# A graph-layer kernel with its ranks moved behind the second filter layer on TensorE, and its places behind the product on VectorE

## What is computed

```
h   = relu(layernorm(x)) @ W_in2f.T
Wij = (smu(edge_attr_20 @ W_f1.T + b_f1) @ W_f2.T + b_f2) * edge_weight[:, None]
agg = segment_sum(h[dst] * Wij, src, num_segments=12500)
out = x + smu(agg @ W_o1.T + b_o1) @ W_o2.T + b_o2
smu(v) = (1.01 v + 0.99 v erf(2.475 v)) / 2
```

## Time and profile before

| | |
|---|---|
| median of 3 runs | 4146.94 us (4142.5 to 4153.49) |
| span of the profiled execution | 5246.4 us |
| TensorE (PE) busy in it | 4105.5 us, 78% |
| VectorE (DVE) busy | 3459.8 us, 66% |
| GpSimd (POOL) busy | 3044.9 us, 58% |
| ScalarE (ACT) busy | 2190.0 us, 42% |
| mean granted TensorE clock | 0.902 of full |

### The profile page before, as it was taken

One profiled execution on the slowest core, in us unless ns is written; L12 is line 12 of the kernel. 1 busy time (PEld: TensorE's weight loads), 2 busy tenths in 40 slices (PEclk: granted clock), 3 DMA queues, 4 the chain that ended last, 5 costly groups with the idle time before them and its releaser, 6 DMA issues.

```text
span 5246.4 us, 97364 instructions
## 1 busy us (share of the span) xinstructions
PE 4105.5 (78%) x23774; PEld 2777.5 (53%) x23774; DVE 3459.8 (66%) x11848; ACT 2190.0 (42%) x7302; POOL 3044.9 (58%) x3173
## 2 busy tenths in 40 slices
PE   6677667777777777777777778788888888887888
PEld 3344335555555555555555555555555666655557
DVE  6666556666666666666666666666666777766677
ACT  4566444444443344444443434434443443334333
POOL 4666655555555555555555555655555555555553
PEclk8888889988988989989889899998888999998999
DMA  6455445554444444444444445554444555554446
GB/s 181 122 147 147 126 118 144 147 144 146 146 133 125 125 124 125 131 127 125 127 126 121 134 145 148 148 153 132 132 133 136 158 157 152 159 160 136 139 137 206
DMA packets 459545, 737.14 MB, mean 141 GB/s; under 512 B 87168, under 2 KB 255466, under 8 KB 459104
## 3 DMA queue, kind: packets, MB, share of 16 engines
q1 hardware_dynamic: 291606, 461.44, 33.5%
q0 software_dynamic: 100000, 206.60, 11.7%
q10 hardware_dynamic: 67626, 65.48, 3.8%
HBM read 465.36 MB, written 267.82 MB: 140 GB/s over the span
## 4 chain that ended last, share of the span: by engine, by line
PE 36%; another core or an unknown queue 25%; DVE 16%; issue 14%; ACT 7%; ACTq 1%; DMA 1%; DVEq 1%; SPq 0%; POOL 0%
PE p_w L1207 7%; PE p_h L1222 7%; PE p_seg L1256 6%; PE p_m L1213 6%; PE p_z L1202 5%; DVE product L1003 4%; DVE hg L995 4%; ACT msg L723 3%; PE p_pos L1244 2%; DVE onehot L988 2%; PE p_pos L1228 2%; DVE act L979 2%; ACT hg L717 2%; DVE pick L983 1%
## 5 line engine op out<-in xcount | busy, mean ns | idle before, releaser
L588 POOL DMA_INDIRECT sorted_rows<-msg,row_idx x3125 | 3004.5, 961 | 2122.6 <-issue 904.5
L1003 DVE CUSTOM_DVE_ANT_0 product<-onehot,p_pos,start_at 128x112 bf16<-128x112 bf16 x3136 | 849.2, 326 | 1096.3 <-remote 1012.3
L723 ACT ACTIVATE msg<-p_m,weight 128x128 f32<-128x128 f32 x3136 | 893.5, 369 | 1439.1 <-remote 786.2
L1256 PEld LDWEIGHTS p_seg<-seg_hot,seg 128*128 128x128 f32 x8288 | 1066.4, 196 | 464.5 <-issue 461.8
L1213 PE MATMUL p_m<-ident,hg 128*128 128x128 f32 x3136 | 561.2, 307 | 905.9 <-DVE hg L995 649.7
L1256 PE MATMUL p_seg<-seg_hot,seg 128*128 128x112 f32 x8288 | 1085.6, 279 | 117.3 <-issue 107.8
L1213 PEld LDWEIGHTS p_m<-ident,hg 128*128 128x128 f32 x3136 | 384.5, 155 | 1102.0 <-DVE hg L995 675.3
L1207 PE MATMUL p_w<-act,w_f 128*128 128x512 f32 x1568 | 932.0, 679 | 10.4 <-issue 5.7
L1202 PE MATMUL p_z<-attr,w_f 128*128 128x512 f32 x1568 | 853.8, 626 | 56.3 <-issue 24.3
L995 DVE SCALAR_TENSOR_TENSOR hg<-p_w,bias_w,hg 128x512 f32<-128x512 f32 x784 | 588.0, 750 | 464.9 <-remote 155.4
L717 ACT COPY hg<-p_h 128x512 f32<-128x512 f32 x784 | 461.9, 589 | 878.4 <-remote 592.3
(11 more groups left out here) (114 smaller groups left out, 2157.8 us busy)
## 6 DMA issues: line engine op xcount, KB each, us to landing
seg<-sorted_rows SPq DMA_DIRECT2D x448, 322.5 KB
seg<-sorted_rows SPq DMA_DIRECT2D x196, 516.0 KB
ends<-ends SPq DMA_DIRECT2D x392, 256.0 KB
sorted_rows<-msg,row_idx POOLq DMA_INDIRECT x3125
sorted_rows<-zero_rows ACTq DMA_DIRECT2D x336, 129.0 KB
win<-h SPq DMA_DIRECT2D x392, 96.0 KB
attr<-in_attrT SPq DMA_DIRECT2D x392, 80.0 KB
seg<-sorted_rows SPq DMA_DIRECT2D x56, 387.0 KB
```

The costliest lines, as they stand in the source:

```text
L588: pool.indirect_dma_start(out=sorted_rows[:, :], out_offset=bass.IndirectOffsetOnAxis(ap=row_idx[:, slot, k:k + 1], axis=0), in_=msg[:, sl ...
L723: last = act.activation(msg[:, slot, k, 0:F], p_m[:, k, :], ACT.Copy, scale=weight[:, bass.ds(n.value(TILES_U, k), 1)])
L1003: last = dve.tensor_tensor_reduce(out=product[:, k, :], in0=onehot[:, slot, k, :], in1=p_pos[:, 0:BUCKETS], scale=1.0, scalar=start_at[:, ...
L1256: last = pe.matmul(out, seg[:, it.slot, l * it.tiles + k, 0:F], seg_hot[:, it.slot, l * it.tiles + k, :], start=(k == 0), stop=(k == it.ti ...
```

## The change

On TensorE `rank(c-1)` goes from ahead of `targets(c-1)` and `filter2(c-1)` to behind them, and a wait for s_w of unit c-1 stands ahead of it: TensorE waits there until the second layer that it has just issued is complete. On VectorE `gather_sum` and `product_of(c-1)` go ahead of `places(c-1)` and `row_numbers(c-1)`. No instruction with work in it is added or removed; 783 beats have the new order (the very first ones are written out apart and stay).

```diff
@@ VectorE, step @@
-                if st.has(1):
-                    places(st.at(1), st.v(1), st.ring(1), st.i is None and st.rnd == 0 and st.c == mid_step + 1)
                 for it in st.items(1):
                     if it.closes:
                         gather_sum(it)
                 if st.has(1):
+                    product_of(st.at(1), st.v(1))
+                    places(st.at(1), st.v(1), st.ring(1), st.i is None and st.rnd == 0 and st.c == mid_step + 1)
                     row_numbers(st.at(1), st.v(1), st.ring(1))
-                    product_of(st.at(1), st.v(1))
@@ TensorE, step @@
                 if st.has(1):
-                    rank(st.at(1), st.ring(1), st.rnd_of(1), st.opens(1))
                     targets(st.at(1), st.pair(1), st.q(1), st.v(1))
                     filter2(st.at(1), st.v(1))
+                    wait_for(pe, s_w, st.at(1), 1, 1)
+                    rank(st.at(1), st.ring(1), st.rnd_of(1), st.opens(1))
```

## The result

The kernel after takes **4156.01 us** (median of 14 runs, 4152.37 to 4161.26) against 4149.12 us for the kernel before in 14 runs: a ratio of **1.0018, 95% interval 1.0011 to 1.0026**. The direction is right, the size is a third of what was forecast.

What follows compares the result with a forecast made beforehand. POOL was taken as the bound, at 5.05 us a unit. To 4147 us came 32 us where PE's beats pass that, less 9 us of lead and 2 us already paid: 4168 us, range 4122 to 4212.

Steps and rivals of the forecast that it cites:

- the floor of 4099 us: Whole run if POOL never waits: 39 us before the first scatter, 3947 of scatters, 113 behind the last.
- The wait's cost: PE's wait between second layer and ranks, in 783 beats: 0.32 us a beat, from 0.20 to 0.45.
- the 0.10 us for the weight load: Part of PE's wait: the ranks' first weight load, 0.10 us ahead of its matmul, is laid bare behind the wait.
- Part 2: New order on PE, ranks behind picked rows and second layer: same matmuls, zero, up to 9 x 0.5 us at round openings.
- The heavy rounds: Seventh and eighth rounds, where PE's beat passes POOL's 5.05 us: 17 us and 15 us.
- The lead that I subtracted: PE's lead over POOL on entering the heavy rounds: covers 9 us of the 32 us excess.
- The gain from the order: Reordering on PE and DVE: both put at zero in the sum.
- faster: Rival: longer lead covers short interruptions, saving half of POOL's 48 us of waits; 4125 us, chance 0.16.
- the 48 us that POOL waits: All waits of POOL before the change: median of 4147 us against 4099 us without waits.
- The gain in lead: Product ahead of row numbers on DVE: PE can run about 3 us further ahead of POOL.
- No change that can be measured: Rival: heavy rounds' 32 us shrink to under 12, within about 0.3%; 4147 us, chance 0.31.
- PE as the bound in most rounds: Rival: a mean clock under about 0.95 lengthens PE's beats; 79 us less 9, 4217 us, chance 0.16.

Runs made afterwards that it cites:

- the slowed GpSimd: Kernel after, with and without TensorE's wait, plus a memset and a wait on GpSimd in each unit: 4748.25 and 4750.6 us, ratios 1.1414 and 1.1421.
- no_wait: Kernel after without TensorE's wait for the second layer, both moves kept: 4138.38 us, ratio 0.9983 to the kernel before.
- wait_heavy: Kernel after with TensorE's wait kept only in the seventh and eighth rounds: 4159.05 us, ratio 1.0006 to the kernel before.
- before_again: Kernel before, unchanged, run again for a second profile: ratio 1.0002, profiled span 4135.8 us.
- dve_only: Kernel before with only the move on VectorE, TensorE's order unchanged and no added wait: 4145.7 us, ratio 0.9998.

## Why the prediction was right or wrong

**The bound was right.** POOL's pitch of 1.263 us, 5.05 us a unit, and the floor of 4099 us came out of a profile that was 26% too long; the clean profiles show the same pitch, and the slowed GpSimd shows the time following it. Taking the durations and not the waits of the first profile was the step that held.

**The wait's cost was too high, and the order's on TensorE was put at zero.** I summed 0.16 + 0.10 + 0.06 = 0.32 us for the wait; measured are 0.22 to 0.23. The term that failed is the 0.10 us for the weight load. The load does start only when the wait is met (3434.05), but the matmul is recorded as starting with it, and the ranks take 0.40 us as before. The Trainium skill, in "TensorE: Matmul & The Clock Gate", section "Step-by-step: what each phase is for", says that TensorE pulls a weight load ahead of matmuls in flight when it goes to the background buffer. By that rule and my other two terms the wait would cost 0.22 us. The number agrees with the trace, but the trace has the load behind the wait and not ahead of it, so it does not show that mechanism. Part 2 gave the new order nothing on TensorE; no_wait shows 0.06 us a beat. The two errors nearly cancel: the eight-tile beat grew by 0.30 us where the sum had 0.32, and that this is close is luck.

**The heavy rounds were mis-sized.** This is the first step that made the forecast too large: TensorE's beat in these rounds was put 0.09 us too long. I had 17 us for the seventh round and 15 for the eighth. The eight-tile beat before is 4.96 us and not 5.03: the transposes of the earlier trace rows, with a wait of TensorE just ahead of them, took 0.49 us, and back to back they take 0.43 or 0.44 (in after from 3437.15 to 3437.58). So the excess over 5.05 us after is 0.21 and not 0.30 us, 12 us in the seventh round; in the eighth, by the medians of its beats (8 of 5.26, 13 of 6.15 and 19 of 4.81 us), the mean is 5.34 us and not 5.43, 11 us. That is 23 us where I had 32. The lead that I subtracted was 9 us; early in the seventh round it is 5.3 us in the trace of after, and the round used it up. With my other terms the sum would have been some 12 us instead of 21. The price of the wait measured by itself is 14.6 us.

By the units' mean lengths in the two profiles (seventh 5.206 before and 5.233 us after, eighth 5.186 and 5.428) the seventh costs 2 us and the eighth 10 us more than before. The split between them is not firm: wait_heavy, with the same order in these rounds, has 5.329 and 5.423. The stop at a late landing just before the eighth round falls into the seventh, with a wait of POOL of 6.5 us in before_again, 3.0 and 2.2 in after, 5.1 in no_wait and 7.3 in wait_heavy. Since after and wait_heavy have the same order and the same wait there, one trace of each can't show that the longer lead shortens it.

**The gain from the order had no term.** This is the second step, a term put at nothing. I put the reordering at zero in the sum and held it for the rival "faster" (4125 us). no_wait shows 7 us of gain, about a seventh of the 48 us that POOL waits, although TensorE's beat is 0.06 us longer in it. 14.6 - 7 = 7.6 us is the measured difference. Where the 7 us arise stays open: POOL's waits over the 0.30 us between scatters add up to 31 us in before_again and 29 in no_wait, and one profile of each, the former of the shortest of its 11 executions, can't tell 5 us. The granted clock is not the reason: its median over the runs is 0.979 before, 0.982 for no_wait and 0.989 for dve_only, which gains nothing.

**The gain in lead was right.** I forecast about 3 us more of it; in the second to fourth rounds p_w is complete a median of 6.1 to 6.3 us before the end of POOL's previous unit, against 3.5 to 3.7 us in before_again. The gain in lead, 2.6 us, is as forecast; the lead with which TensorE enters the heavy stretch of the seventh round was not (5.3 us where I subtracted 9).

**The rivals.** "No change that can be measured" had the right range (within 12 us), by a mixture I had not named: a wait of 0.22 us paid in two rounds, and a gain from the order. PE as the bound in most rounds is refuted: the granted clock is 0.98 to 0.99 of full in the clean profiles, not the 0.87 to 0.90 of the earlier trace rows, which went with the stops of that one execution. The agreement of that rival with the 48 us left over was a coincidence. In before_again 31 us of them are waits of POOL (12 in the first round, 14 in the two heavy rounds, 5 elsewhere) and some 11 us are scatters that follow each other a little later than 1.263 us; the rest lies between this execution and the median. What I had not thought of is that the two moves depend on each other: either side's effect alone is no guide to both (1.0174 and 0.9998 make 1.0018).

## What to carry to other kernels

Find the engine whose instructions stand back to back, and price every change by what it does to that engine's waits: a wait of 0.22 us in 783 beats costs nothing that can be measured in 687 of them and 14 us in the 96 where the beat is as long as the bound. Work out beat lengths round by round, since the length of most beats (4.6 against 5.05 us here) hides the rounds that pay, and take them from beats that follow each other without idle time: the 0.06 us by which one beat was read too long was a fifth of the excess. When work is moved later on one engine, look for what stands ahead of the critical instruction on the engine that consumes it: the ranks behind the second layer cost 1.7% until the product had been moved ahead of the places.

## What the runs showed of the hardware

One profiled execution was 26% longer than the timed ones, with GpSimd's durations right and the waits wrong, and with a lower TensorE clock (0.902); a second profile of the same kernel was within 0.3% of the timed runs, at 0.982. TensorE waiting for its own matmul of 512 columns loses 0.22 us; a second such wait, ahead of the first layer, 0.26 us. With the ranks ahead of it instead of the second layer, the first layer holds TensorE 0.06 us longer (0.92 us to the sums instead of 0.86). Scatters of 128 rows issued by GpSimd follow each other at 1.263 us in all these kernels, and a small memset with a wait ahead of four of them adds 0.74 us, of which 0.22 are the memset. Right after some thousand packets under 512 B on another queue, packets of scatters took 0.57 to 0.76 us instead of 0.09.
